# Top-2 experts block: the first W1 weights issued by GpSimd at the block's begin, no longer by SyncE behind constants and stored rows

## The reference, cut to what matters

```python
logits = jnp.einsum('bsh,eh->bse', x, Wr)
probs = jax.nn.softmax(logits, axis=-1)
top_v, top_i = jax.lax.top_k(probs, K)            # K = 2
top_v = top_v / jnp.sum(top_v, axis=-1, keepdims=True)
for e in range(E):                                # E = 8, H = 512, M = 2048
    w_e = jnp.sum(jnp.where(top_i == e, top_v, 0.0), axis=-1)
    h = jax.nn.gelu(jnp.einsum('bsh,mh->bsm', x, W1[e]) + b1[e], approximate=False)
    y = jnp.einsum('bsm,hm->bsh', h, W2[e]) + b2[e]
    out = out + y * w_e[..., None]
```

## Time and profile before

| what | value |
|---|---|
| median of 3 runs | 2726.27 us |
| profiled execution's own time | 2734.06 us |
| its span | 2732.3 us |
| TensorE busy | 2451.3 us (90% of the span) |
| mean granted TensorE clock | 0.946 |
| the last block's front, from its barrier to the first up product | 2171.8 to 2207.4 us |

### The profile page before, as it was taken

How to read it: one execution, slowest core, us unless ns; L and a number is a source line. 1 busy time by engine, 2 the same in 40 slices (tenths; PEclk the granted TensorE clock), 3 DMA queues, 4 the chain that set the end, 5 groups by cost and what they waited for, 6 DMA issues and landing times. The chain is left out here.

```text
span 2732.3 us, 31769 instructions
## 1 busy us (share of the span) xinstructions
PE 2451.3 (90%) x11965; PEld 1237.7 (45%) x11965; DVE 1380.3 (51%) x1954; ACT 918.0 (34%) x1860; POOL 645.1 (24%) x523
## 2 busy tenths in 40 slices
PE   7899999889999999897599799886997779999997
PEld 4344444334555555545345454353664423333332
DVE  5689999521778886731435512286445521111114
ACT  3555565303533334501122110086333312222221
POOL 0477887501000000001201100000000024444342
PEclk9899999999999999998789899998998889999998
DMA  3632222335535444334610000012000162560534
GB/s 106 201 105 89 78 83 91 97 124 212 179 126 179 158 150 116 131 116 175 210 57 0 24 19 3 26 69 93 1 1 4 47 258 88 205 272 26 240 108 145
DMA packets 96588, 301.31 MB, mean 110 GB/s; under 512 B 27018, under 2 KB 57447, under 8 KB 81725
## 3 DMA queue, kind: packets, MB, share of 16 engines
q1 hardware_dynamic: 62784, 171.06, 18.8%
q0 software_dynamic: 33664, 128.35, 12.9%
HBM read 446.13 MB, written 47.22 MB: 181 GB/s over the span
## 5 line engine op out<-in xcount | busy, mean ns | idle before, releaser
L749 POOL TENSOR_TENSOR x_rows<-ms_state,mb_C_everywhere 128x800 f32<-128x800 f32 x128 | 247.1, 1937 | 167.0 <-DVE ms_state L719 134.9
L774 PE MATMUL psum<-mb_context,mb_key_w 128*128 128x361 f32 x768 | 271.0, 492 | 14.7 <-ACT x_rows L633 8.5
L1005 PE MATMUL psum<-at_Wv,at_context 128*128 128x512 f32 (+1 forms) x576 | 265.0, 599 | 0.0
L719 DVE TENSOR_TENSOR_SCAN ms_state<-ms_decay,psum 128x800 f32<-128x800 f32 x128 | 233.0, 1820 | 19.1 <-ACT ms_decay L666 14.3
L3079 ACT ACTIVATE tf_hidden<-psum,tf_b 128x64 f32<-128x64 f32 x512 | 111.7, 329 | 364.0 <-PE psum L3035 364.0
L3024 PE MATMUL psum<-tf_W,tf_x_T 128*64 128x512 f32 x1024 | 231.1, 599 | 0.8 <-DVE tf_x_T L3088 0.8
L3046 PE MATMUL psum<-tf_W,tf_hidden 128*64 128x512 f32 x1024 | 226.8, 595 | 0.0
L774 PEld LDWEIGHTS psum<-mb_context,mb_key_w 128*128 128x128 f32 x768 | 141.0, 194 | 148.1 <-issue 44.5
L2959 POOL DMA_INDIRECT tf_W<-in_L_W,tt_weight_row x120 | 119.4, 995 | 179.9 <-PE psum L3024 122.3
L1106 ACT ACTIVATE at_prob<-psum,at_neg_max 100x722 f32<-100x722 f32 x128 | 110.4, 863 | 144.9 <-DVE at_neg_max L1168 144.8
L1168 DVE TENSOR_REDUCE at_neg_max<-psum 100x1 f32<-100x722 f32 x128 | 115.5, 903 | 79.6 <-PE psum L1026 79.3
(11 more groups left out here) (479 smaller groups left out, 3828.5 us busy)
## 6 DMA issues: line engine op xcount, KB each, us to landing
at_piece<-in_L_W_f POOLq DMA_DIRECT2D x24, 1024.0 KB, 6.4
keys_dram<-x_rows SPq DMA_DIRECT2D x128, 180.5 KB, 1.9
at_k_cols<-keys_dram SPq DMA_DIRECT2D x64, 361.0 KB, 3.2
sf_W<-in_L_W SPq DMA_DIRECT2D x16, 1024.0 KB, 6.5
tf_W<-in_L_W SPq DMA_DIRECT2D x8, 2048.0 KB, 21.4
mb_context<-in_ctxT SPq DMA_DIRECT2D x16, 541.5 KB, 4.6
at_context<-in_ctxT SPq DMA_DIRECT2D x8, 1083.0 KB, 5.0
ternary_dram<-at_piece_made POOLq DMA_DIRECT2D x14, 512.0 KB, 4.0
```

Of the source, the lines that this page charges most:

```text
L719: nc.vector.tensor_tensor_scan(state[:, n % RH, :], decay[:, g % RA, :, :].rearrange("p b l -> p (b l)"), drive, 0.0, ALU.mult, ALU.add).t ...
L749: nc.gpsimd.tensor_tensor(seen[:, n % RV, :], state[:, n % RH, :], cC[:, n, :], ALU.mult).then_inc(weighed, 1)
L774: last = nc.tensor.matmul(side("key", u, t == KE - 1)[:, 0:SH], lhsT=wk[:, k, e * P:(e + 1) * P], rhs=keys[:, h, k, :], start=(k == 0), st ...
L1005: last = nc.tensor.matmul(bank[0:rows_of(t), :], lhsT=ctxT[:, b % 2, k, t * P:t * P + rows_of(t)], rhs=wv[:, k, h * BANK:(h + 1) * BANK], ...
```

## The change

Nothing is computed otherwise. The four DMAs of the first pair's W1 are taken out of SyncE's program (where they stood behind ten small DMAs and the store of the rows) and put at the head of GpSimd's program in this block, ahead of its first wait. They keep their order, sizes, destinations and semaphores. They also change queue: from q1 to q0.

```diff
+    of_first = lambda a, z: a[FIRST[z] * P:(FIRST[z] + 1) * P, :]
+
     def sync(sp):
-        of_first = lambda a, z: a[FIRST[z] * P:(FIRST[z] + 1) * P, :]
-        for h in range(2):
-            for z in range(2):
-                sp.dma_start(w1_half(z, h), of_first(dram[f"L1_W1_{h}"], z)).then_inc(w1_first[h], 16)
         for z in range(2):
             sp.dma_start(b1[z][:, :], of_first(b1_rows, z)).then_inc(b1_first, 16)
         sp.wait_ge(x_loaded[0], 16)
...
+        for h in range(2):
+            for z in range(2):
+                pool.dma_start(w1_half(z, h), of_first(dram[f"L1_W1_{h}"], z)).then_inc(w1_first[h], 16)
         pool.wait_ge(table_ready, 1)
         pool.wait_ge(x_stored, 16)
         take_x(0)
```

## The result

| | before | after |
|---|---|---|
| median of the runs of this comparison | 2732.40 us (7 runs, 2725.27 to 2736.95) | 2742.59 us (7 runs, 2734.84 to 2750.57) |
| span of the profiled execution | 2732.3 us | 2741.1 us |

The ratio is 1.0040, 95% interval 1.0024 to 1.0055: 0.0040 x 2732.4 = 10.9 us slower (6.6 to 15.0). The forecast time, 2741.0, is close and the sign is right, but the path is that of the first rival: `tr_Wr` escaped, and the eight constants were caught.

What follows compares the result with a forecast made beforehand. The last block's front was taken as bound by the chain of constants, count, VectorE's routing and gather, not W1. tr_Wr +19.7 and gather -4.9 gave +14.8 us on the median 2726.27, so 2741 us, range 2726 to 2748.

Steps and rivals of the forecast that it cites:

- the first rival: Last block's front: tr_Wr escapes W1, the constants don't; count +11.3, gather -4.9, sum +6.4 us, 2733 us; chance 0.27.
- What bounds, and that W1 was never waited for: Last block's front: TensorE waits for gather (9.6 us), routing (8.0) and tr_Wr (4.0), none for W1; issuing it earlier buys nothing.
- One packet of each queue in turn, however small: DMA engines: with both queues loaded, each small packet costs a whole packet of the other queue, 0.611 us for W1's 16 KB.
- bunches: Rival, DMA engines: small pieces pass W1 in one turn per DMA and engine; 3.1 - 4.9 = -1.8 us, 2724 us; chance 0.08.
- W1 level with or just ahead of `tr_Wr`, so +19.7 us: Block's begin: W1 arrives at 2173.1, holds tr_Wr's 33 packets per engine, and tr_Wr lands 19.7 us later.
- The constants hide behind `tr_Wr`: Ahead of the count: the other constants find W1 gone, pass in 3.7 us, and are wanted 9.1 us after tr_Wr.
- the upper bound of the forecast: W1's transfer: at 8.28 MB in 22.2 us it takes 2.9 us longer, making the sum +17.7 us.
- SyncE's issuing: SyncE's queue: its 6.58 us of issuing W1 goes, unwaited for; stalls could add 1 to 3 us to the constants' case.
- The gather, -4.9: First gather, last block: with W1 through, it takes 3.4 us instead of 8.28, a gain of 4.9 us.
- Everything behind moves as a block: Behind the gather: all keeps its distances, the down products find W2 no later, TensorE's clock in the front unchanged; no added time.
- The sum: Whole kernel: +19.7 us for tr_Wr and -4.9 for the gather make +14.8 us, 2741 us; chance 0.57.

Runs made afterwards that it cites:

- 4 KB: Changed kernel with each of the four W1 DMAs cut into four of 512 KB, so packets are 4 KB instead of 16 KB; ratio 1.0004 to the kernel before.
- each quarter: Changed kernel with only three, or two, of the four W1 DMAs at the block's begin, the rest behind the first gather; ratios 1.0022 and 1.0027 to the kernel before.
- packed: Eight constants laid in one DRAM tensor, sent as one DMA: in the changed kernel ratio 0.9998, in the kernel before 0.9987, both against the kernel before.
- `tr_Wr` second: Changed kernel with SyncE issuing tr_rank first and tr_Wr after it; ratio 1.0040 to the kernel before.
- issued third: Changed kernel with SyncE issuing tr_Wr behind tr_rank and tr_upto; ratio 1.0066 to the kernel before, median 2751.21 us.

## Why the prediction was right in sum and wrong in a step

In short: the sign and the time came out right, the path did not, and that the time is so close is luck.

**What bounds, and that W1 was never waited for**: right. No wait for W1 appears in either kernel's front, and its earlier issue bought nothing.

**One packet of each queue in turn, however small**: right once both queues are loaded, and the root of all else. It is 430 against 431 over 16 us in the changed kernel, 412 against 408 with 32 B pieces, and the hold shrinks with the size of W1's pieces (4 KB: -9.4 us), their number (-5.0 and -5.2 for each quarter) and the number of pieces held (packed: -14.0). It does not hold for W1's first packets: 336 of SyncE's small ones pass beside 8 of them with `tr_Wr` second, and for 3 us after 2170.8 it is 12 against 64 in the changed kernel.

The Trainium skill (DMA: Bandwidth & Descriptors, Queues, rings and completion order) has an engine drain a whole packet, typically 9 to 17 descriptors, before it switches. Where both queues are loaded for long these traces are against that for SyncE's small pieces, and the time that the forecast worked out for bunches (one turn for each DMA), 2724, is 18.6 us off.

**W1 level with or just ahead of `tr_Wr`, so +19.7 us**: this is the step that failed. The engines met the barrier together, but GpSimd's first issue of the block stands 0.50 us behind SyncE's (2168.34, 2167.84), some 0.6 us behind the end of its own wait (2167.7). So the queues do not start at the same moment, as the kernel's description has it. The forecast took SyncE's 0 and GpSimd's 0 as the same moment, from the end of GpSimd's wait, and put W1's bytes 0.1 us ahead of `tr_Wr`'s; they came at +1.97, 1.47 us behind the issue and not 1.2, and 0.65 us behind `tr_Wr`'s (+1.32). `tr_Wr` needs only 0.5 us of DMA time, so a shift of half a microsecond decides over 20. The experiments bracket it: caught at an issue 0.73 us later, not at 0.36, or, counted against the first issue of W1, caught 0.23 us behind it and not 0.14 ahead. Whether the level start of the forecast would have been enough lies between the two and stays open. A step with such an edge should not have carried 0.57 of the chance on a start time known to half a microsecond; the case with the escape was written down, with 0.27.

**The constants hide behind `tr_Wr`**: followed from the failed step and failed with it. They were caught in its place: +15.3 on the count. The rival had +11.3 for this. It is 4.0 us short: W1 ran some 23.4 us from its first byte to its last landing instead of 20.2 (its last issue at 2170.1, with the longest landing of 23.1 us, is in at 2193.2, or +25.4), and started near +2.0 instead of +1.2. That rate is about the upper bound of the forecast (the rate of the earlier trace rows), which I had given only to the case of `tr_Wr`. It is no cost of the turns: in the kernel before, W1 and the rows move as fast over 16 us, from 2180 to 2196, as W1 beside the constants did from 2174 to 2190 (6.26 MB):

```profile
q1 hardware_dynamic: 428, 6.29, 98.2%
```

That is 0.67 us for a piece of 16 KB in both. The 0.611 of the earlier trace rows came from 6 faster us of that stretch.

**SyncE's issuing**: I had 1 to 3 us of stalls as a possible cost; the two issues of b1 took 14.76 us, and cost nothing, since what stands behind them, the first W2, waits for the gather until 2212.18 anyway.

**The gather, -4.9**: right in mechanism, -4.5 measured (3.78 instead of 3.4).

**Everything behind moves as a block**: nearly. +0.7 us on top for the clock, so +11.5 at the last down product. The ratio says +10.9.

**The sum**: +14.8 forecast, +15.3 - 4.5 + 0.7 = +11.5 by the trace. It came close because the hold ends with W1, whichever piece it catches: with `tr_Wr` caught (issued third) the count was 22.8 us late, with the constants alone 15.3. The forecast had 19.7 for the first, too little by 3, so that the wrong step (7.5 us too much) and the short hold (3.1 too little) partly cancelled. The forecast's own base was the median 2726.27; the kernel before has since run at 2732.3 to 2734.6, and +14.8 on that would have been 2747. So the agreement of 2741.0 with 2742.6 owes some 6 us to the base, against the 4 us that the increment was too large: luck, as said.

## What to carry to other kernels

Before you move a large load into a second DMA queue, count the packets of what the first queue still has to bring for the critical path: each of them, even one of 4 or 32 B, then costs one packet of the large load (0.62 to 0.67 us at 16 KB here), until the load is through. Few large pieces for the constants (packed in one tensor) or smaller pieces for the load (4 KB) take most of that away; so does putting the load behind the constants in the same queue, as the kernel before did. And where a burst of small packets and the begin of a load lie within half a microsecond of each other, forecast both outcomes as nearly equal, since an issue 0.37 us later was worth 22 us of wait here. In all of these runs the large load was GpSimd's and the small pieces SyncE's; the two the other way round, or both from other engines, were not tried.

## What the runs showed that I had not expected

- SyncE's issuing takes long while the small pieces of its queue are held: 14.76 us for two DMAs of 8 KB in the changed kernel, 2.40 in the kernel before. With `tr_Wr` third it strikes earlier, in the timeline of that kernel:

```profile
2171.18 1.99 SPq L2801 DMA_DIRECT2D tr_upper_half<-in_upper_half  x1
2173.20 4.83 SPq L2801 DMA_DIRECT2D tr_block_of_turn<-in_block_of_turn  x1
2178.07 4.29 SPq L2801 DMA_DIRECT2D tr_token<-in_token_of_choice  x1
2182.40 4.31 SPq L2802 DMA_DIRECT2D tt_x_dram<-x_rows  x1
```

- In one queue a gather behind a large load is worse off than beside it: 11.99 us against 8.28, both issued at +25.3. Beside it the gather landed at +33.6, 6 us before the last W1 DMA (+39.6); behind it, only after that one (+37.2 and +36.6).
- From one execution to the next, the begin of this block scatters by 12 us (2164.2 to 2176.2) and the part behind the last down product takes 27.8 to 33.4 us, in no relation to what was changed. That is the noise in which a front's 1 us is lost, and why positions within the block tell more than spans.
- What stays open: why q1 gets next to nothing in the first 3 us of W1, why 16 KB pieces take 0.61 us in one stretch and 0.67 in a longer one, and why freeing the engines by 3 us (packed) did not shorten the gather by itself. None was tried further.
